# An attention and mixture-of-experts kernel on one core: GpSimd's buffer clears are placed behind the first normalisation, and the router's weights are loaded ahead of the large input groups

## The reference

```python
xn = layernorm(x)                       # over the 256 channels, no weights
# banded attention: 32 heads of 8, window 8
q, k, v = split(xn @ qkv_w.T)
attn = where(m != 0, (q @ k.T) * scale * m, -inf)   # m: band with falling weights
s = softmax(attn) @ v @ proj_w.T + proj_b
# mixture of 8 experts, one for each token, and a shared expert
logits = xn @ router_w
e, score = argmax(logits), sigmoid(max(logits))
moe = down[e](silu(gate[e](xn * score)) * up[e](xn * score))
shared = (silu(xn @ sgate) * (xn @ sup)) @ sdown
out = x + s * silu(moe + shared)
```

## Time and profile before

| what | value |
|---|---|
| time, median of 3 runs | 599.69 us (599.25 to 600.19) |
| time of the profiled execution | 600.95 us |
| its span, first to last instruction | 599.1 us |
| TensorE busy | 546.0 us, 91% of the span |
| VectorE busy | 439.2 us, 73% |
| GpSimd busy | 255.5 us, 43% |
| ScalarE busy | 240.3 us, 40% |
| mean granted clock of TensorE | 0.976 of full |

### The profile page before, as it was taken

The page is one execution under the profiler, slowest core; times in us unless marked ns, Lnnn a source line. Parts: engine busy times, 40 slices in busy tenths (PEclk is TensorE's granted clock), DMA queues, the critical chain, the costliest instruction groups (busy, mean ns, idle before and its releaser), DMA issues.

```text
span 599.1 us, 10330 instructions
## 1 busy us (share of the span) xinstructions
PE 546.0 (91%) x3302; PEld 474.1 (79%) x3302; DVE 439.2 (73%) x1029; ACT 240.3 (40%) x506; POOL 255.5 (43%) x188
## 2 busy tenths in 40 slices
PE   1989999979988999999999999999999999898952
PEld 1757789858867899989899988899879788786941
DVE  6777858898768557566566466646899999999862
ACT  1464454536652443442433433342535434352210
POOL 7133324038885223223323322320476795974630
PEclk9989999989998999999999999999999999999977
DMA  9624534235625666766566756563235664754421
GB/s 302 208 80 156 187 106 124 88 96 176 186 95 166 202 188 200 217 189 197 174 189 199 219 175 204 156 171 102 44 63 74 92 89 60 104 76 64 70 44 19
DMA packets 106345, 83.17 MB, mean 139 GB/s; under 512 B 42164, under 2 KB 104500, under 8 KB 106164
## 3 DMA queue, kind: packets, MB, share of 16 engines
q1 hardware_dynamic: 90180, 64.81, 36.9%
q0 software_dynamic: 10496, 12.59, 12.7%
q10 hardware_dynamic: 5616, 5.11, 2.5%
HBM read 59.41 MB, written 27.26 MB: 145 GB/s over the span
## 4 chain that ended last, share of the span: by engine, by line
PE 60%; DVE 13%; POOL 8%; issue 6%; DMA 5%; ACT 4%; SPq 1%; ACTq 0%; POOLq 0%; DVEq 0%
PE psV L939 11%; PE psM L989 11%; PE psS L914 8%; PE psM L998 5%; PE psM L966 5%; PE psM L925 4%; PE psM L961 4%; PE psM L889 4%; DMA xnT<-ys_dram,slot 4%; PE psM L894 3%; POOL xnT L442 3%; POOL Sx L432 3%; PE psM L947 2%; DVE O L760 2%; DVE Sx L708 2%
## 5 line engine op out<-in xcount | busy, mean ns | idle before, releaser
L432 POOL TENSOR_TENSOR Sx<-Sx,mx 128x752 f32<-128x752 f32 x64 | 100.6, 1571 | 122.5 <-DVE mx L718 122.1
L939 PE MATMUL psV<-VB,PTs 128*128 128x132 f32 x1024 | 134.8, 285 | 17.8 <-DVE O L760 17.6
L939 PEld LDWEIGHTS psV<-VB,PTs 128*128 128x128 f32 x1024 | 129.2, 195 | 22.4 <-issue 21.0
L426 POOL TENSOR_TENSOR Sx<-Sx,cst 128x752 f32<-128x752 f32 x28 | 47.0, 1677 | 183.4 <-DVE Sx L708 183.4
L914 PE MATMUL psS<-kBD,qBD 128*128 128x188 f32 x512 | 97.8, 323 | 0.2 <-DVE Sx L708 0.2
L914 PEld LDWEIGHTS psS<-kBD,qBD 128*128 128x128 f32 x512 | 84.7, 190 | 9.6 <-issue 2.5
L740 DVE STREAM_TRANSPOSE PTs<-Sx 128x512 f32<-128x512 f32 x128 | 82.8, 685 | 4.2 <-ACT Sx L497 4.2
L708 DVE TENSOR_TENSOR Sx<-psS,cst 128x752 f32<-128x752 f32 x64 | 60.0, 938 | 30.6 <-PE psS L914 30.2
L989 PE MATMUL psM<-xT,EB 128*128 128x128 f32 x624 | 76.5, 276 | 0.6 <-DMA EB<-in_L_ffn_up_w 0.6
L760 DVE TENSOR_TENSOR O<-psV,rs 32x128 f32<-32x128 f32 x256 | 73.5, 287 | 4.8
L989 PEld LDWEIGHTS psM<-xT,EB 128*128 128x128 f32 x624 | 73.8, 192 | 3.0 <-ACT qBD L486 1.3
(11 more groups left out here) (106 smaller groups left out, 688.6 us busy)
## 6 DMA issues: line engine op xcount, KB each, us to landing
EB<-in_L_ffn_gate_w SPq DMA_DIRECT2D x39, 256.0 KB, 3.1
EB<-in_L_ffn_up_w SPq DMA_DIRECT2D x39, 256.0 KB, 3.6
EB<-in_L_ffn_down_w SPq DMA_DIRECT2D x39, 256.0 KB, 3.0
VB<-v_dram SPq DMA_DIRECT2D x256, 32.0 KB
stage<-xs_dram SPq DMA_DIRECT2D x39, 128.0 KB, 2.2
ys_dram<-yb ACTq DMA_DIRECT2D x39, 128.0 KB, 3.1
xs_dram<-blank SPq DMA_DIRECT2D x9, 512.0 KB, 3.2
v_dram<-vS SPq DMA_DIRECT2D x8, 512.0 KB, 3.0
```

The lines of the kernel that those rows point to most:

```text
L432: nc.gpsimd.tensor_tensor(s, s, mx[n % 3][:, :].unsqueeze(2).broadcast_to([P, 2 * G, KW]), ALU.subtract).then_inc(a_sub, 1)
L939: last = mm(psV[:, j, at:at + HS * VW], PTs[n % 2][:, k, j, i, :], VB[n % 2][:, i, k, :, VW * j:VW * j + VW], start=k == 0, stop=k == 1)
```

## The change

Three edits. The router's weights are issued directly behind the q, k, v weights, ahead of the four later groups of `X`. GpSimd clears only the first `kBD` at once; then it waits until `n_xn` is 2, which is when the four tiles of the first sequence are normalised, and clears the rest. `s_zero` now counts to 3: to 2 when both `kBD` are clear, to 3 when all is. The waits of SP and VectorE that stood for everything go to 3; that of ScalarE in `qk_out` stays at 2. Last, VectorE writes the two columns of ones in `VB` with one memset for each head where there were two.

```diff
                     sp.dma_start(wqkv[:, :, 0:3 * C], wqkv_d.rearrange("(k p) f -> p k f", p=P)).then_inc(s_wq, 16)
+                    sp.dma_start(wqkv[:, :, 3 * C:], router_w.rearrange("(k p) f -> p k f", p=P)).then_inc(s_wr, 16)
             for dst, src in ((wsgu[:, :, 0:F], sgate_w), (wsgu[:, :, F:2 * F], sup_w), (wsdn[:, :, :], sdown_w)):
                 sp.dma_start(dst, src.rearrange("(k p) f -> p k f", p=P)).then_inc(s_ws, 16)
-            sp.dma_start(wqkv[:, :, 3 * C:], router_w.rearrange("(k p) f -> p k f", p=P)).then_inc(s_wr, 16)
             sp.dma_start(wp[:, :, :], wproj_d).then_inc(s_ws, 16)
...
-            sp.wait_ge(s_zero, 2)
+            sp.wait_ge(s_zero, 3)
             sp.wait_ge(s_one, 1)
...
-            for i in range(2):
-                zero(kBD[i][:, :, :, :], 0.0)
+            zero(kBD[0][:, :, :, :], 0.0)
+            pool.wait_ge(n_xn, 2)
+            zero(kBD[1][:, :, :, :], 0.0).then_inc(s_zero, 1)
             for v in VB:
                 zero(v[:, :, :, :, :], 0.0)
...
-                    dve.wait_ge(s_zero, 2)
+                    dve.wait_ge(s_zero, 3)
...
-            dve.wait_ge(s_zero, 2)
+            dve.wait_ge(s_zero, 3)
             for v in VB:
                 for h in range(HS):
-                    for c in (0, 2 * VW - 1):
-                        ins = nc.vector.memset(v[QB * h:QB * h + QB, :, :, h, c:c + 1], 1.0)
+                    ins = nc.vector.memset(v[QB * h:QB * h + QB, :, :, h, 0:2 * VW:2 * VW - 1], 1.0)
             ins.then_inc(s_one, 1)
```

## The result

| | before | changed |
|---|---|---|
| median of 6 runs | 599.53 us (598.53 to 600.19) | 596.13 us (595.15 to 597.45) |
| profiled execution, its time | 600.95 us | 597.45 us |
| its span | 599.1 us | 595.6 us |

The ratio is 0.9942, with a 95% interval of 0.9923 to 0.9961. In a second set on another occasion it was 0.9933 (0.9912 to 0.9953). The gain is 3.4 us, forecast 3.3; by the first interval it lies between 2.3 and 4.6 us.

What follows compares the result with a forecast made beforehand. TensorE was taken to bound the kernel, started late by VectorE's first normalisation. Five stalls, 0.73 + 0.70 + 0.71 + 0.51 + 0.66 = 3.31 us, off the 599.69 us median gave 596.4 us, range 595.0 to 598.3.

Steps and rivals of the forecast that it cites:

- The stalls: Opening, VectorE's first normalisation: five steps that wait for GpSimd instructions run free, 3.31 us in all off the chain.
- TensorE's start: Opening: TensorE's first matmul moves from 12.70 to 9.39 us, with nothing else holding it.
- GpSimd's moved list: Clears and casts behind the normalisation: 8.0 us from 9.8, casts ending at 17.8, at no cost.
- Rival 3: Opening: moved clears hold up VectorE's moments, whole gain gone, 600.0 us; chance 0.03.
- The router's load: Load queue: moved early, it gains nothing by itself and delays later groups of X by 0.3 us, at most 0.75.
- left in place the load would take back 3.2 of the 3.3: Ahead of the v projection: an unmoved router's load, landing at 21.8, would cost 3.2 us of the gain.
- The v projection: TensorE's opening: it follows the k projection at 18.6 us without a wait.
- rival 1: First q matmuls: TensorE's clock rises at the same wall time, gain only 1.65 us, 598.0 us; chance 0.08.
- VectorE's cover: Ahead of weigh(0): VectorE's slack shrinks from 4.0 to 0.8 us, with the ones taking 0.45, at worst 0.88.
- Rival 2: Opening: VectorE becomes the bound ahead of weigh(0), some 597.2 us; chance 0.05.
- The lead runs through: Everything after weigh(0): tied to work, not wall time, so the 3.31 us lead lasts to the end.
- Rival 5: Thin stretches: TensorE's clock falls more often, 1.65 us each, 601.3 us with three more; chance 0.03.

Runs made afterwards that it cites:

- experiment 3: Kernel before with the router's load moved and the clears of VB and Sx, at their old place, cut into quarters: ratio 0.9976.
- experiment 4: Kernel before with the router's load moved and only GpSimd's two casts put behind the normalisation: trace only, not timed, weigh(0) at 26.66 us.
- experiment 2: Kernel before with only the router's load moved: ratio 0.9994.
- experiment 1: Changed kernel with the router's load put back behind the shared expert's weights: ratio 1.0039, 601.49 us.
- experiment 5: Changed kernel measured once more, nothing altered: ratio 0.9933 against the kernel before.
- experiment 8: Changed kernel with scores(0) ahead of the last value tile, the other 28 tiles' variance ahead of weigh(0), the ones behind it: ratio 0.9897, 594.06 us.

## Why the prediction was right

- **The stalls.** The sum was 3.31 us. The normalisation started 3.37 us earlier, of which 0.04 are the earlier landing of `X` (4.32 against 4.36): 3.33. Experiments 3 and 4 show the mechanism piece by piece: short memsets end the waits beside the memsets, moving the cast ends that of L636. The sum held for the profiled execution. It is no constant of the kernel before: experiments 2 and 4 had the long memsets too, and `weigh(0)` at 26.02 and 26.66, largely since a difference of 0.2 us or less in when the steps begin decides which memset each meets. That the medians differ by 3.40, within 0.1 of the sum from one trace, is partly luck: the second set has 4.25 us (600.15 and 595.90).
- **TensorE's start** was forecast at 9.39 and was 9.33.
- **GpSimd's moved list** was to end by 18 and ended at 17.62, and the moments beside it kept their pace: 0.34 us a tile (2.71 for 8 from 12.61) against 0.33. Rival 3 falls.
- **The router's load.** Its price on `X` was taken as 0.3 us. The third large group landed 0.27 later in the changed trace than before, but this is within the scatter: the last 12 tiles start between 17.96 and 18.91 in the eight traces with the load moved, and at 18.27 in experiment 1, where it was not. So the price is not measured. A delay of 1.5 us, as priced for twice the packets, is not to be seen in any of them. The step that was mis-sized is "left in place the load would take back 3.2 of the 3.3": experiment 1 took back 4.86. Of this 3.82 are the wait (21.89 against 18.07), more than forecast because TensorE came to the v projection earlier than 18.6, and 1.04 the slower v projection behind it, because the wait also brought TensorE's clock down: 5.49 us, against 4.45 in the changed kernel, where a wait for ScalarE is part of it. I priced the wait and not what the idle time does to the work behind it.
- **The v projection** stood at 18.07, not 18.6. The k projection went faster (2.64 us against 2.98). None of that arrived, as the last value tile waited for ScalarE's copies of k. I had read TensorE as the chain of the opening; its last third was ScalarE's copies, in both kernels. It did not matter for the sum, since the copies start with the end of the q projection and so moved by the same amount, 19.21 to 15.84, 3.37 us. By this reading rival 1 is wrong in its price, since a clock that rises late costs only in what comes ahead of those copies. When the clock rose can be told only from the matmuls' times: the profile's clock column reads 1.00 from 15 to 18 us of the kernel before, where the first q matmuls last up to 767 ns.
- **VectorE's cover** was put at 0.8 us and was 0.40. The moments ended as forecast (22.6 and 22.65); the eight memsets of ones took 0.84 us, near the bound of 0.88 and not the 0.45 that I took. In the second trace of the changed kernel (experiment 5) the cover was gone and VectorE released `weigh(0)`, 0.2 us late. Rival 2 is thus real in its mechanism, at a price of 0.2 us in one trace of two; by the prediction's own sign ("`weigh(0)` is released by VectorE's own work") it was wrong there.
- **The lead runs through** to the end, as said: 3.37 us at `weigh(0)`, 3.5 in the span, with excursions of up to 1.4 us between. No rival is needed for the time. Rival 5, more falls of the clock, is there in both signs. Its price of 1.65 us for each stretch was an upper bound: the stretch it was read from cost nothing, and the one at n = 60 cost 1.2.

What stays open: the lead jumps from 2.79 to 4.08 between n = 32 and 33. The clock is 1.00 there in both; TensorE waited once in the kernel before, 1.04 us at 348.76 for VectorE's `ehT`, and not in the changed one. Followed back, `ehT` was late because ScalarE was: its DMA issue for `ys_dram` took 1.77 us at 342.56 before and 0.38 at 339.77 in the changed kernel, while SP's issue beside it took 1.75 and 0.42. Why those issues took longer is open. At which end on GpSimd a waiting step is let in (experiment 4) was seen once and not tried by itself.

## What to carry to other kernels

A chain of tiny VectorE steps beside long GpSimd instructions pays up to one such instruction for each step, and in one case two; look for small operations whose ends coincide with ends on GpSimd, and move the long work behind the chain or cut it into short pieces, which did the same here. When a chain is pulled forward, list every load that had landed just in time for it: one 8 KB load left behind turned a gain of 3.4 us into a loss of 1.7, since the wait of 4.3 us also brought TensorE's clock down to half behind it. A chain that names TensorE for a run of matmuls can hide a wait inside the run, so the weight loads' waits have to be read too.

## What the runs showed of the hardware

- A `TENSOR_SCALAR` or `COPY` step on VectorE (0.17 us free) took 0.68 to 0.97 us beside a memset, but not every operation with one input is held: a `RECIPROCAL` took 0.18 beside the cast (at 10.13, before), and the moments kept 0.34 to 0.35 us a tile beside memsets. A two-input addition went through a memset in 0.16 us, while others took 0.83 beside a cast and 1.67 beside an addition on GpSimd. The page "SBUF — State Buffer" of the Trainium skill (Who interferes with whom) says that a two-input operation contends only with a GpSimd instruction that reads SBUF; these rows agree (the 0.90 us of L626 were spent in the queue behind L625).
- A waiting step can be passed over: 1.91 us, through the whole of two memsets, where 0.04 us later the same step waited for one (0.97).
- A stretch of TensorE at half clock cost 1.2 us at n = 60 (6.51 against 5.30 us) and nothing at n = 1 (8.71 against 8.70).
- VectorE's own memset of the ones was not held up by GpSimd's addition (0.84 us at 24.59, beside the addition from 24.74, in experiment 8). Eight memsets of two columns cost as much as sixteen of one: 0.84 against 0.88 us.
